# POOL casts P ahead of the residual sum, and the low part of v moves from DVE to POOL, in a group-norm attention kernel

## The reference, cut to what matters

```python
def _gn(v, G=32, eps=1e-5):            # v: B, H, W, C
    g = v.reshape(B_, H_, W_, G, C_ // G)
    m = jnp.mean(g, axis=(1, 2, 4), keepdims=True)
    s = jnp.var(g, axis=(1, 2, 4), keepdims=True)
    return ((g - m) / jnp.sqrt(s + eps)).reshape(v.shape)

qkv = jnp.einsum('bglc,dc->bgld', x, W_qkv) + b_qkv      # x is _gn(x) here
score = jnp.einsum('bghlc,bghmc->bghlm', q, k) / scale   # scale = C ** 0.5
score = jax.nn.softmax(score, axis=-1)
out = jnp.einsum('bghlm,bghmc->bghlc', score, v)
return x + out
```

## Time and profile before

| | us |
|---|---|
| median of 3 runs | 4224.27 |
| lowest, highest run | 4221.31, 4226.06 |
| the profiled execution's own time | 4225.53 |
| its span in the trace | 4223.5 |
| granted TensorE clock in it, mean | 0.992 of full speed |

### The profile page before, as it was taken

The page is one execution under the profiler, slowest core; times in us unless marked ns, Lnnn a source line. Parts: engine busy times, 40 slices in busy tenths (PEclk is TensorE's granted clock), DMA queues, the critical chain, the costliest instruction groups (busy, mean ns, idle before and its releaser), DMA issues.

```text
span 4223.5 us, 147348 instructions
## 1 busy us (share of the span) xinstructions
PE 3958.7 (94%) x44133; PEld 2923.8 (69%) x44133; DVE 3759.4 (89%) x7138; ACT 3125.2 (74%) x8193; POOL 2134.7 (51%) x3089
## 2 busy tenths in 40 slices
PE   4999999899999999999999899999999999999998
PEld 3767777677776777767777677776767777677776
DVE  6998989889898898988989889898898989989887
ACT  3777777677776777767777677776777777777776
POOL 1555555455554555545555455554555555555554
PEclk9999999999999999999999999999999999999999
DMA  7999898998998989989899998989989998997878
GB/s 197 198 193 201 196 198 196 191 188 199 195 199 181 193 199 198 198 179 200 194 199 198 180 199 197 197 198 181 197 195 201 196 197 193 197 192 166 165 164 167
DMA packets 2438095, 809.81 MB, mean 192 GB/s; under 512 B 2175232, under 2 KB 2437760, under 8 KB 2437760
## 3 DMA queue, kind: packets, MB, share of 16 engines
q1 hardware_dynamic: 2311040, 679.97, 79.7%
q10 hardware_dynamic: 126720, 125.84, 10.7%
HBM read 134.42 MB, written 134.22 MB: 64 GB/s over the span
## 4 chain that ended last, share of the span: by engine, by line
issue 41%; POOL 26%; DVE 15%; POOLq 5%; PE 5%; DVEq 4%; ACT 2%; DMA 1%; SPq 0%; ACTq 0%
POOL p_hi L600 21%; DVE o_norm L455 9%; POOL x_ring L607 4%; POOLq L156 2%; DVEq L460 1%; PE o_bank L315 1%; DVE neg_max L429 1%; POOL y_ring L616 1%; ACT prob L394 1%; PE qk_bank L277 1%; DVE p_lo L436 1%; PE s_bank L299 1%; DVE v_lo L442 1%; POOLq L616 1%; POOLq L607 1%
## 5 line engine op out<-in xcount | busy, mean ns | idle before, releaser
L616 POOL TENSOR_TENSOR y_ring<-image,o_norm 128x256 f32<-128x256 f32 x1024 | 744.5, 727 | 2015.7 <-DVE o_norm L455 2009.9
L394 ACT ACTIVATE prob<-s_bank,neg_max 128x256 f32<-128x256 f32 x4096 | 1604.4, 481 | 189.8 <-issue 177.2
L375 ACT ACTIVATE qk<-qk_bank,b_in 128x256 f32<-128x256 f32 x2048 | 861.0, 472 | 757.2 <-PE qk_bank L277 755.6
L436 DVE SCALAR_TENSOR_TENSOR p_lo<-prob,p_hi 128x1024 f16<-128x1024 f32 x1024 | 1254.3, 1225 | 174.9 <-POOL p_hi L600 144.6
L429 DVE TENSOR_REDUCE neg_max<-s_bank 128x2 f32<-128x512 f32 x2048 | 1309.7, 681 | 35.8 <-PE s_bank L299 35.8
L299 PE MATMUL s_bank<-qk 64*128 64x256 f32 x8192 | 1172.1, 404 | 30.9 <-issue 30.0
L277 PE MATMUL qk_bank<-xc,w_norm 128*128 128x256 f32 x4096 | 1164.2, 407 | 0.0
L600 POOL TENSOR_SCALAR p_hi<-prob 128x1024 f16<-128x1024 f32 x1024 | 1071.4, 1046 | 22.8 <-ACT prob L394 18.1
L277 PEld LDWEIGHTS qk_bank<-xc,w_norm 128*128 128x128 f32 x4096 | 697.1, 190 | 394.9 <-issue 327.0
L299 PEld LDWEIGHTS s_bank<-qk 64*128 64x128 f32 x8192 | 709.4, 187 | 253.2 <-issue 205.3
L315 PE MATMUL o_bank<-v_hi,pt_lo 128*128 128x65 f16 x8192 | 852.9, 193 | 26.6 <-issue 18.0
(11 more groups left out here) (72 smaller groups left out, 2449.4 us busy)
## 6 DMA issues: line engine op xcount, KB each, us to landing
out_dram<-y_ring SPq DMA_DIRECT2D x512, 256.0 KB, 2.5
image<-in_x_dram ACTq DMA_DIRECT2D x240, 512.0 KB, 4.3
pt_hi<-p_hi SPq DMA_TRANSPOSE x1024, 3.3
pt_lo<-p_lo SPq DMA_TRANSPOSE x1024, 3.1
image<-in_x_dram SPq DMA_DIRECT2D x4, 2048.0 KB, 16.2
w_in<-in_L_conv_W_qkv_dram SPq DMA_DIRECT2D x1, 192.0 KB, 2.3
b_in<-in_L_conv_b_qkv_dram SPq DMA_DIRECT2D x3, 0.5 KB, 2.1
```

The source lines that it names most:

```text
L375: ins = act.activation(qk[:, v % 2, t, :], qk_bank[:, t * TOK:(t + 1) * TOK], ACT.Identity, bias=b_in[:, t:t + 1])
L394: ins = act.activation(prob[:, m, c:c + TOK], s_bank[m][h][:, a * TOK:(a + 1) * TOK], ACT.Exp, bias=neg_max[:, m, h, a:a + 1])
L436: dve.scalar_tensor_tensor(out=p_lo[:, v % 2, :], in0=prob[:, v % 2, :], scalar=P_SCALE, in1=p_hi[:, v % 2, :], op0=ALU.mult, op1=ALU.subt ...
L616: pool.tensor_tensor(y_ring[:, m, :], image[:, par, bass.ds(row, 1), :].rearrange("p a c -> p (a c)"), o_norm[:, v % 2, :, :].rearrange("p ...
```

## The change

- POOL's list becomes p_high of u, v_low of u, refill of u+6, finish of u-4.
- v_low is a POOL stage. It reads a float32 copy of v in SBUF, the new tile v_full (two buffers), and v_hi.
- ACT's v_high issues two instructions: the copy of the bank to v_full, ahead of it a wait for vlo_done of two rows back (that buffer of v_full is read), and the cast to v_hi as before.
- PE's project_v waits for vhi_done of the row before in place of vlo_done.
- DVE's list becomes p_low of u-2, sums of u-4, next_image(0), next_image(1), divide of u-4, next_image(2), row_max twice, next_image(3) and measure.

```diff
+        v_full = sb("v_full", [P, 2, J, HEADS, HC])
...
             def project_v(base, v, at):
                 if not known_below(base, 1 - v):
-                    pe.wait_ge(vlo_done, base + v)
+                    pe.wait_ge(vhi_done, base + v)
...
-                act.activation(v_hi[:, v % 4, :, :, 0:HC],
-                               v_bank[:, 0:J * C].rearrange("p (j h c) -> p j h c", j=J, h=HEADS),
-                               ACT.Copy).then_inc(vhi_done, 1)
+                bank_view = v_bank[:, 0:J * C].rearrange("p (j h c) -> p j h c", j=J, h=HEADS)
+                if not known_below(base, 2 - v):
+                    act.wait_ge(vlo_done, base + (v - 1))
+                act.activation(v_full[:, v % 2, :, :, :], bank_view, ACT.Copy)
+                act.activation(v_hi[:, v % 4, :, :, 0:HC], bank_view, ACT.Copy).then_inc(vhi_done, 1)
...
-            def v_low(base, v, at):
-                dve.wait_ge(vhi_done, base + (v + 1))
-                dve.tensor_tensor(v_lo[:, v % 4, :, :, 0:HC],
-                                  v_bank[:, 0:J * C].rearrange("p (j h c) -> p j h c", j=J, h=HEADS),
-                                  v_hi[:, v % 4, :, :, 0:HC], ALU.subtract).then_inc(vlo_done, 1)
...
             def order(run, next_image):
+                run(-2, p_low)
                 run(-4, sums)
                 next_image(0)
-                run(-2, p_low)
                 next_image(1)
+                run(-4, divide)
                 next_image(2)
-                run(-4, divide)
-                run(-1, v_low)
                 run(0, row_max, 0)
...
+            def v_low(base, v, at):
+                pool.wait_ge(vhi_done, base + (v + 1))
+                pool.tensor_tensor(v_lo[:, v % 4, :, :, 0:HC], v_full[:, v % 2, :, :, :], v_hi[:, v % 4, :, :, 0:HC],
+                                   ALU.subtract).then_inc(vlo_done, 1)
...
             def order(run, next_image):
+                run(0, p_high)
+                run(0, v_low)
+                run(+6, refill)
                 run(-4, finish)
-                run(+5, refill)
-                run(-1, p_high)
```

## The result

The changed kernel takes 4954.2 us (median of 4 runs, 4936.8 to 4969.0) against 4223.5 before: ratio 1.173, 95% interval 1.171 to 1.176. The forecast was 4100, in a range up to 4280. The profiled execution took 4968.96 us, with a span of 4967.1.

What follows compares the result with a forecast made beforehand. It took a DVE and POOL ring of 3.93 us a step as the bound. From 4225.5 us it took 768 x (3.99 - 3.85) = 108 and 90 x 0.20 = 18, giving 4100, range 4000 to 4280.

Steps and rivals of the forecast that it cites:

- SP's queue: On SP, transpose_high(u-1) is issued behind store(u-6), which now waits for a finish ending POOL's step; no cost in the forecast.
- rival 3: Store waits for finish, delaying transpose_high and p_high: 3.86 us a step, 4.11 with slow landings, 4345 us; chance 0.09.
- The sum: Whole-kernel total: 108 us saved in 768 steady steps, 18 in 90 statistics steps, 0 in the last ten: 4100 us.
- The old ring: DVE and POOL work from p_lo through o_norm, y_ring, x_ring, p_hi back to p_lo: 3.93 us, setting the step before.
- The steady step: Average step in the 768 steady steps: from 3.99 us to 3.85, saving 108 us.
- The six statistics rows: Rows 48 to 53, with statistics on DVE: 4.30 us a step before, 0.20 less forecast, 18 us over 90 steps.
- The last ten: Last ten steps of an image, 150 in all: 3.92 us each, forecast to gain 0.
- p_low's missing wait for the cast: On DVE, p_low would no longer wait for POOL's cast of P; the 0.03 to 0.2 us there go.
- Turns: p_lo on DVE and POOL instructions alternate at SBUF: p_lo lengthens POOL's round by 1.14 - 0.15 at best, 3.72 a step.
- Rival 1: PE becomes the bound as p_lo and POOL overlap at half speed: POOL 3.30 us a step, 4005 us total; chance 0.18.
- rival 2: p_lo and POOL instructions wait for each other fully, nothing hidden: 4.13 us a step, 4365 us total; chance 0.13.
- PE's floor: Distance between scores on PE without the v matmuls' wait for v_lo: 3.77 us a step.

Runs made afterwards that it cites:

- run 1: The changed kernel with the store of a row pair issued one step later (lead -7 in place of -6): 4059.1 us, ratio 0.961.
- run 4: The changed kernel with p_low as a tensor_reduce over prob alone, one SBUF input instead of two: 4598.0 us, ratio 1.089.
- run 3: The kernel before with only v_low moved to POOL, reading v_full, and the old orders otherwise kept: 4662.2 us, ratio 1.104.
- run 11: The changed kernel with the store at lead -7 and p_low as a one-input tensor_reduce over prob: 3933.1 us, ratio 0.932.
- runs 8 and 9: The changed kernel with POOL's list p_high, finish, v_low, refill: 4047.7 us (8); the same plus the store at lead -7: 4010.4 us (9).

## Why the prediction was wrong

**The step that failed** is the line "SP's queue" with rival 3, the store's ring. The sum gave it nothing, and the rival had 0.09 and, at its worst, 4.11 a step. Measured are 4.94 in the image above, and run 1 shows that this is the whole miss: with the store a step later and all else as changed, the kernel takes 4059, where the sum said 4100. The rival had the place right (the store waits for a finish at the end of POOL's step, and transpose_high stands behind it). It was too small for these reasons:

- It followed transpose_high into p_high only. The next transpose_low stands in the same queue, 3.14 us late in the timeline, and values on PE wait for it: 604.5 us. I had checked what each SP instruction waits for, and not who else is queued behind it. The slack that pt_lo had before was never put into a number. The sign given for this rival, p_hi waiting for DMA pt_hi in every second step, came in every fourth (260 times); with quarter loads it is 452 times.
- It took the landing as 3.3, or 4.3 at worst. Behind a load it was 5.2. With quarter loads the loss is 470 us smaller. Load and transpose are issued 0.16 us apart at both ends of the round shown, which looks like both following the same late step; no run moved the load's issue.
- It left PE out of the ring, its idle time and its clock. The clock of the round was 0.83, and eight scores took 2.03. The turn of p_lo, on the other hand, it had: 1.14, where x_ring lost 1.00 in the round shown. Without turns the loss is 356 us smaller (run 4). What the clock alone costs no run separates.

**What held.**

- The old ring. It is gone from the chain, and p_high no longer waits behind y_ring.
- The steady step, forecast 3.85 with SP's queue free: 3.84 in run 1. The mean agrees, in part by luck (below). The six statistics rows, 4.30 - 0.20 = 4.10: 4.20 in the image shown. The last ten, 3.92 unchanged: 3.77 there.
- v_low on POOL at 0.67 from start to start: 0.60 in run 1 (2397.80 to 2398.40, where x_ring starts), 0.66 recorded. v_full at 0.40: 0.39. p_low's missing wait for the cast: 13.6 us in all in run 1, but 176.9 in the changed kernel.
- "refill one row further ahead", zero: x_ring's wait for PE is 35.8 us in the kernel after and 36.0 in run 1, nearly all of it one wait at the start.
- Turns, "at best by 1.14 - 0.15". The 0.15 hidden at the edge came back in run 3 (0.59 shared, 0.44 lost; half speed would have cost 0.30, and v_lo was no longer than alone), so it was the wait and not half speed. Rival 1's mechanism falls with that, and so does rival 2's price of nothing hidden. The Trainium skill, SBUF — State Buffer, section Who interferes with whom, has the rule with its condition of two SBUF inputs; runs 4 and 11 agree, y_ring never above 0.74 us beside a p_lo of one input, and up to 1.81 in run 1 with two.

**Luck in the steady step.** The sum set 3.99, which holds the loop ends, against 3.85, which like the old ring's 3.93 does not; with 0.06 for them the forecast would have been 3.91 a step, 46 us more. And POOL's round with its turn is 3.65 where POOL never idles, shorter than the sum's best case of 3.72. The timeline of run 1:

```profile
2396.79 1.04 POOL L596 TENSOR_SCALAR p_hi<-prob 128x1024 f16<-128x1024 f32 x1
...
2397.80 0.66 POOL L601 TENSOR_TENSOR v_lo<-v_full,v_hi 128x256 f16<-128x256 f32 x1
...
2398.40 0.40 POOL L608 COPY x_ring<-image 128x256 f32 x1
2398.53 1.35 DVE L439 SCALAR_TENSOR_TENSOR p_lo<-prob,p_hi 128x1024 f16<-128x1024 f32 x1
2398.76 1.72 POOL L617 TENSOR_TENSOR y_ring<-image,o_norm 128x256 f32<-128x256 f32 x1
...
2400.44 1.04 POOL L596 TENSOR_SCALAR p_hi<-prob 128x1024 f16<-128x1024 f32 x1
```

In the first sixteen steps of the image shown for run 1, most are near 3.65 and every fourth is 3.99 or more; in those with a measurement they go from 3.0 to 5.0. Only their mean met the forecast.

**Left out** was a wait of divide. It needs y_done of two rows back, and with the finish last in POOL's step it has to wait for it: 376.0 us in the changed kernel and 334.2 in run 1, in 490 waits, and none in runs 8 and 9.

**PE's floor** was mis-sized: 3.77 forecast, 3.63 in run 11. The 1.07 from q and k to v was the scores' distance; measured is 0.96, which is 0.11 of the 0.14. The rest is open.

**The chances.** 0.09 for a ring through SP was too little for a queue in which one instruction's wait moved from the head to the end of another engine's step. The rows had the warning: my own sum for it was 3.86 a step, equal to the forecast, so there was no margin in it for a slower landing.

## What to carry to other kernels

When an engine's list is reordered, go through every queue that waits for a moved instruction, and ask of each who stands behind the waiting one, and what slack those have in us; a DMA queue worked in order passes a wait on to transfers that have nothing to do with it. A ring whose own sum equals the forecast is not a side case: price it with the longest landing that a neighbour can cause. And try the cheap repairs (a lead, the order of two issues) before judging the change: here they turned 17% slower into 5% faster.

## What the runs showed of the hardware

- A VectorE instruction with two SBUF inputs and a GpSimd instruction took turns: the later one was longer by the time shared less about 0.15 us (run 3, v_lo and p_lo: 0.59 shared, 0.44 lost; x_ring 1.40 in the changed kernel and y_ring 1.72 in run 1 behind p_lo, against 0.40 and 0.73 alone). A tensor_reduce of the same 1024 elements with one input did not lengthen them: in run 11, 205 of the 210 y_ring between 1000 and 1800 us lie beside it for over 0.2 us, and none of its 1024 took over 0.74.
- A transposing DMA issued 0.16 us behind a 512 KB load landed after 5.2 us, against a median of 3.2 over the kernel. One of run 1, issued at 2403.88 and 1.79 us behind a load, took 6.77, and PE waited 2.0 us for it: the slow landing is there without the held queue too, in a kernel of 4059 us.
- After 2.73 us without work PE ran at a granted clock of 0.50 for the 5.8 us that follow, and eight scores took 2.03 us.
